# A decoder kernel's gated feed-forward: gate and up from split one-pass parts, the weight parts made in the stage before it and streamed by tile, and the scan's C rows spread from one 128-row tile

## The reference, cut to what matters

```
w = lut[idx]                                    # gate, up and down each look their weights up
gate = x @ w_gate.T;  up = x @ w_up.T           # 512 -> 1376
h = silu(gate) * up
out = h @ w_down.T                              # 1376 -> 512

state = state * exp(delta_t * A) + (delta_t * u_t) * B_t      # 16 states x 512 channels, 512 steps
y_t = sum over n of state[n] * C_t[n]
```

## Time and profile before

| | us |
|---|---|
| median of 3 runs | 2576.68 (2576.60 to 2576.71) |
| the profiled execution, its own time | 2584.38 |
| its span, first to last instruction | 2582.6 |
| context stage in that span | 930 to 1198 |
| feed-forward and scan | 1198 to 1865 |

### The profile page before, as it was taken

How to read it: one execution, slowest core, us unless ns; L and a number is a source line. 1 busy time by engine, 2 the same in 40 slices (tenths; PEclk the granted TensorE clock), 3 DMA queues, 4 the chain that set the end, 5 groups by cost and what they waited for, 6 DMA issues and landing times. The chain is left out here.

```text
span 2582.6 us, 24445 instructions
## 1 busy us (share of the span) xinstructions
PE 2262.6 (88%) x6992; PEld 1049.2 (41%) x6992; DVE 1771.1 (69%) x2979; ACT 920.4 (36%) x1759; POOL 1052.6 (41%) x789
## 2 busy tenths in 40 slices
PE   6998998999899777774798989989869999999858
PEld 3554444455455443332243434334333333434224
DVE  1887687688768877773688897987745455554454
ACT  1443323334333323331554636446203323232311
POOL 2453333355333424443598888988700000000033
PEclk9999999999999988886899999999979999999878
DMA  6000000000000022225321222221142222121021
GB/s 245 18 21 17 17 25 21 17 17 21 21 17 25 22 88 82 82 82 198 116 91 53 86 83 82 91 77 62 49 131 50 50 49 49 40 58 34 16 98 53
DMA packets 88746, 158.34 MB, mean 61 GB/s; under 512 B 14912, under 2 KB 42432, under 8 KB 86352
## 3 DMA queue, kind: packets, MB, share of 16 engines
q1 hardware_dynamic: 72256, 139.76, 17.1%
q10 hardware_dynamic: 15888, 17.43, 2.1%
q0 software_dynamic: 512, 0.13, 0.0%
HBM read 101.18 MB, written 30.80 MB: 51 GB/s over the span
## 5 line engine op out<-in xcount | busy, mean ns | idle before, releaser
L1389 PE MATMUL c_bank<-c_xn_t,c_weights 128*128 128x512 f32 (+1 forms) x704 | 326.4, 609 | 21.1 <-ACT c_h_t L1429 19.5
L706 POOL TENSOR_SCALAR a_prob<-a_prob,a_rsum 128x256 f32<-128x256 f32 x256 | 147.1, 594 | 466.8 <-DVE a_rsum L634 466.6
L1287 DVE TENSOR_TENSOR_SCAN s_state<-s_decay,s_state 128x512 f32<-128x512 f32 x256 | 305.0, 1210 | 36.1 <-ACT s_decay L1221 36.1
L1237 POOL TENSOR_TENSOR s_state<-s_b_rows,s_delta_u 128x1024 f32<-128x1024 f32 x128 | 301.2, 2363 | 11.2 <-DMA s_b_rows<-scan_bc 8.8
L1221 ACT ACTIVATE s_decay<-s_delta,s_a 128x512 f32<-128x512 f32 x256 | 173.2, 688 | 296.5 <-DVE s_state L1287 269.4
L438 PE MATMUL a_bank<-a_xn_t,a_wq 128*128 128x512 f32 x512 | 227.2, 592 | 0.0
L521 PE MATMUL a_bank<-a_wo,a_out_t 128*128 128x512 f32 x512 | 222.3, 592 | 0.0
L1910 POOL DMA_DIRECT2D d_qs<-d_neg_t x16 | 8.2, 514 | 515.3 <-DVE d_neg_t L1841 515.3
L549 ACT ACTIVATE a_prob<-a_score,a_neg_m 128x256 f32<-128x256 f32 x256 | 117.8, 476 | 278.8 <-DVE a_neg_m L629 278.6
L320 DVE TENSOR_SCALAR f_picks<-f_mask,f_lut_xor,f_lut 128x260 int32<-128x260 int32 x512 | 202.5, 468 | 9.6 <-DVE f_mask L314 1.1
L1762 ACT ACTIVATE d_prob_t<-d_score 128x512 f32<-128x512 f32 x256 | 139.0, 595 | 194.5 <-PE d_score L1645 193.2
(11 more groups left out here) (194 smaller groups left out, 3726.6 us busy)
## 6 DMA issues: line engine op xcount, KB each, us to landing
s_b_rows<-scan_bc SPq DMA_DIRECT2D x64, 512.0 KB, 3.6
f_idx<-in_idx SPq DMA_DIRECT2D x64, 130.0 KB, 2.1
ffn_weights<-f_picks SPq DMA_DIRECT2D x64, 130.0 KB, 1.8
...
d_qs<-d_hi SPq DMA_DIRECT2D x128, 64.0 KB, 2.0
d_ks<-d_hi SPq DMA_DIRECT2D x128, 64.0 KB, 2.0
...
```

Of the source, the lines that this page charges most:

```text
L1237: pool.tensor_tensor(self.state[:, s], row.broadcast_to([P, 2, T]), self.delta_u[:, h % 2], ALU.mult) \
L1287: dve.tensor_tensor_scan(self.state[:, s, e, :], self.decay[u % 2][:], self.state[:, s, e, :], 0.0, ALU.mult, ALU.add).then_inc(self.scann ...
L1389: mm = nc.tensor.matmul(banks[b][0:width[o], :], weights[:, lo:lo + width[o]], xn_t[:, k, :], start=(k == 0), stop=(k == KD - 1))
```

## The change

1. **Parts of the weights.** A class `WeightSplit` runs in the context stage. The 11008 gate and up columns are cut into 16 pieces of 688, four in each pass. For each: SP loads it, ACT rounds it to float32r (`hi`), POOL subtracts (`lo`), SP stores both to two new DRAM tensors. Pieces 0 and 1 of a pass stand on ACT between the copies of the attention and the SiLU of `u`, on POOL between the factor adds and `d_u`; pieces 2 and 3 stand on both at the end of the pass. On SP the loads of 0 and 1 stand behind the factors' loads, and the stores of 2 and 3 at the end, ahead of the next pass's factors. To make room, `one_e` now lies in `conv`, and `delta` in `log1p`.
2. **Fills.** x is split the same way (ACT rounds out of PSUM, DVE subtracts). A fill is twelve float32r matmuls: for each k, hi x hi, hi x lo and lo x hi; lo x lo is left out. The weights of a tile `o` come as two DMAs of 512 KB into one of four slots, the first by SP, all others by ACT, in each of the four passes anew: `load_ahead` behind each `gate`. The down weights stay in SBUF in float32 as before, from one DMA.
3. **Order of the pieces.** The features of the next pass move from piece 34 to piece 28, between the second and the third down tile; the statistics and the normalization move to pieces 8 and 12, among the fills. The last down tile's add comes at the end of the pass.
4. **C.** All four batches' C rows, twice, are loaded into one 128-row tile at the stage's start by eight DMAs, rounded and split once; `spread_c` picks one of 64 columns. The split in each pass is gone.

The diff, cut to its core:

```diff
+class WeightSplit:
+    PER_PASS = 4
+    SW = W_DOWN // (B * PER_PASS)
...
+    def load(self, sp, i, n):
+        if n >= 2:
+            sp.wait_ge(self.subtracted[n % 2], self.turn(i, n))
+        sp.dma_start(self.raw[:, n % 2, :].bitcast(I32), self.scratch["weights"][:, self.columns(i, n)]) \
+            .then_inc(self.raw_in[n % 2], 16)
+    def round(self, act, i, n):
+        act.wait_ge(self.raw_in[n % 2], self.turn(i, n) * 16 + 16)
+        act.wait_ge(self.stored[n % 2], self.turn(i, n) * 32 + 1)
+        self.nc.scalar.copy(self.hi[:, n % 2, :], self.raw[:, n % 2, :]).then_inc(self.rounded[n % 2], 1)
...
 def stage_context ... sync
+                split.load(sp, i, 0)
+                split.load(sp, i, 1)
...
+                for n in range(2):
+                    split.store(sp, i, n)
+                    split.load(sp, i, n + 2)
...
+                for n in range(2, 4):
+                    split.store(sp, i, n)
 stage_ffn
-    STATS_AT, NORM_AT = FILLS + 2, FILLS + 6
+    XN_AT = FILLS + 2 * PARTS
+    STATS_AT, NORM_AT = 8, 12
...
-                for k in range(KD):
-                    lo = b * W_UP + k * INTER + o * P
-                    mm = nc.tensor.matmul(banks[b][0:width[o], :], weights[:, lo:lo + width[o]], xn_t[:, k, :],
-                                          start=(k == 0), stop=(k == KD - 1))
+                terms = [(k, w, x_) for k in range(KD) for w, x_ in ((0, 0), (0, 1), (1, 0))]
+                for k, w, x_ in terms:
+                    at = (b * KD + k) * width[o]
+                    mm = nc.tensor.matmul(banks[b][0:width[o], :], w_parts[:, n % SLOTS, w, at:at + width[o]],
+                                          xn_parts[:, x_, k, :],
...
+            for n in range(1, SLOTS):
+                load_ahead(n)
             scan.scalar_setup(act)
             features(0)
-            for o in range(EARLY, OT):
-                load_weights(act, o)
+            act.dma_start(w_down[:].bitcast(I32), ...)
...
                     if j < FILLS and j % 2 == 1:
                         gate(i, j // 2)
+                        if i * OT + j // 2 >= 1:
+                            load_ahead(i * OT + j // 2 + SLOTS - 1)
 class Scan
-        self.nc.tensor.matmul(self.c_bank[c % 2][:], self.c_pick[:, n:n + 1].broadcast_to([2 * DS, P]),
-                              self.c_parts[:, i % 2, :], start=True, stop=True).then_inc(self.c_spread, 1)
+        self.nc.tensor.matmul(self.c_bank[c % 2][:], self.c_pick[:, n:n + 1].broadcast_to([P, P]),
+                              self.c_parts[:], start=True, stop=True).then_inc(self.c_spread, 1)
```

199 lines of the change are left out of this document (125 added, 74 removed).

## The result

| | us (median) | us (range) | profiled execution: us / span |
|---|---|---|---|
| before | 2576.69 | 2576.60 to 2577.45 | 2584.4 / 2582.6 |
| after | 2531.85 | 2530.08 to 2534.32 | 2532.93 / 2531.1 |

The ratio is 0.983 (95% interval 0.981 to 0.984): 44.8 us faster. I had forecast 19.5 us. The two traces differ by more, 51.5 us of span, because the profiled execution before lay 7.7 us over its median and the one after 1.1 over. No view shows what the 7.7 us are, but the clock goes with them: of the other executions of the kernel before on record, those of 2582 us and more had a mean granted clock of 0.935 to 0.938, those under 2580 one of 0.938 to 0.942, and the profiled one had 0.937. All of the 51.5 us lie in the two changed stages (943.1 us before, 891.5 after).

The account below looks back on a forecast made before the run. PE bounds the fills, POOL and DVE close behind. Start -23.3, pass 0 +1.6, passes 1 and 2 -2.5 together, pass 3 -8 make -32; context +12.5; total -19.5 from 2576.7, 2557 us, range 2522 to 2582.

Parts of the forecast that it names:

- The start: Start of the feed-forward: ACT issues one load before the first decay, not eighteen; first scan 23.3 us earlier.
- Context: Context stage: weight split adds 12.5 us, +2.5 in three passes, +2 in the first, +3 for last stores.
- The norm among the fills: Fills: normalization 7.4 and statistics 3.6 make 11 us of DVE; 3 us more for the clock, in each of three passes.
- Stalls at the gates: Fills: DVE stands still 1.15 us at 28 gates, 0.7 from the table loads' chain and 0.4 from DMA issues.
- The downs: Down stretch of a pass: 50.9, plus 3 for features and 3.6 of PE idle, 57.5 us against 62.9.
- PE's piece: Fills: twelve matmuls in 2.82 us and a spread of 0.24; a piece falls from 4.05 to 3.06 us.
- DVE's waits for a fill: Start of a pass's fills: PE needs 6.4 us before the first lift, DVE has 4.1 of work, 2.3 idle.
- the full gain: Rival, chance 0.14: gate stalls don't appear in the fills, ACT running ahead; 32 us less, 2525 us.
- Context eats it: Rival, chance 0.10: rounding late in all context passes, +29 in place of 12.5, fills gain 4 less; 2578 us.
- A fall of the clock: Rival, chance 0.05: PE's granted clock falls to 1.2 GHz among fills, half the pieces slow, 79 us more; 2636 us.
- the held issues: Rival, chance 0.09: ACT's DMA issues behind gates held by a full queue, 1.4 us more a pair; 2600 us.

Follow-up runs that it names:

- the best with three terms: Changed kernel with GpSimd's factor sums, then subtractions of pieces 0 and 1 behind d_u, ScalarE's roundings behind the SiLU, factor sum stored from ScalarE's queue: 2491.35 us, 0.965.

## Why the prediction was wrong

The direction and the range held (2522 to 2582), the size didn't: 44.8 us, not 19.5. By the stage marks the change brings -51.7 where -19.5 was forecast, and the difference lies in pass 0 (-7.2, forecast +1.6) and passes 1 and 2 (-30.9 together, forecast -2.5); the start and the context stage were each worse than forecast, by 2 and 6. So the steps that failed are those of a pass: the norm's length, the stalls at the gates and the downs. By the prediction's own steps:

- **The start, -23.3.** Measured -21.3 (42.5 to 21.2). Right, within 2. POOL got its B rows 18.7 us after the stage's start, behind the 4 MB of weights, where 17 was forecast.
- **Context, +12.5.** Measured +18.3: passes +0.9, +3.8, +5.2, +4.4 and the end +4.0. The mechanism was named, and two of its operations were in the wrong place: I let two subtractions hold the convolution at its start for 1.7 us (it was 0.4) and overlooked that the other two stand right behind the factor sums, at the convolution's end, and hold it for 2 x 1.4 us. ACT's rounding ended at 1095.06 in pass 2, where the forecast had 1091 "just in time"; the last SiLUs waited for DVE all the same.
- **The norm among the fills, 11 us and 3 for the clock.** This step failed worst. I took 7.4 us from the earlier trace rows as the operations' length. It was 1.9 of work and 5.5 of being held beside GpSimd's operations, and the earlier trace rows had shown me just that one stage earlier. Measured 1.9 and 2.5, with the small operations some 4.9 in all: 6 us less in each of three passes. That GpSimd rests at piece 12 was luck: the prediction didn't look, and at piece 16 it doesn't. The clock I had half right. Three passes have a norm among their fills, 0 to 2. In pass 0 the granted clock fell to 1.2 GHz twice for 3.4 us, each time within 1 us of the end of a pause of PE (2.4 and 2.1 us) at the norm's two places; over the fills of pass 0 it was 0.94. In passes 1 and 2 PE paused as long, and the clock stayed at 1.00: 3 us less in each of the two.
- **Stalls at the gates, 1.15 us at 28.** The tables' part was right (0.7, measured 0.7); the issues' 0.4 was not (most issues are done ahead of the gate, as ACT's timeline and the run with twice the issues show), and 17 gates had a stall, not 28. 12.5 us in place of 32; and by the run without tables only 3 to 8 of these 12.5 were on the path.
- **The downs, 57.5.** Measured 53.3, since the C spread saves 0.39 us twelve times, 4.7 us, and I had given it nothing there. The idle time of PE for the features' subtraction was 3.3 us (forecast 3.6). The last pass's downs had nothing of the saving: 51.9, forecast 50. There PE waited 2.8 us for a weighing and the granted clock lay at 1.2 GHz for 6.8 us.
- **PE's piece.** 12 matmuls follow each other in 2.8 us, as forecast, but with the spread behind them a piece takes 3.3 to 3.5 us from start to start at most places and not 3.06. Here 3.53:

```profile
1420.80 2.96 PE L1460 MATMUL c_bank<-c_xn_parts,c_w_parts 128*128 128x512 f32 x12
1423.82 0.50 PE L1242 MATMUL s_c<-s_c_parts,s_c_pick 128*128 128x512 f32 x1
1424.33 3.04 PE L1460 MATMUL c_bank<-c_xn_parts,c_w_parts 128*128 128x512 f32 x12
```

  What makes the difference of 0.2 to 0.5 is open. And the statement "PE is the engine to relieve" with three terms as the means was half of it: the cheaper spread alone brings the float32 piece from 4.05 to 3.66 us, and DVE and the gates need about that.
- **Against it**, DVE's waits for a fill didn't go: 5.5 us in the fills of passes 1 to 3 and 11.4 in pass 0, where I had 2.3.

For passes 1 and 2: 157.5 forecast, 143.3 measured. Of the 14.2, norm 6, clock 3, stalls 4 (6.9 less 2.9), downs 4.2, less 3 for the waits. Of the rivals, the full gain (2525) came nearest. Its reason, stalls that don't appear, held for 20 of its 32 us; the rest came from the norm and the downs, which it didn't name, and was partly eaten by the waits for PE, so that its figure is near by luck. "Context eats it" had the direction of that stage's error right (18.3, between 12.5 and 29). A fall of the clock over much of the fills was seen only with one term, and the held issues only with loads over 43 and 42 partitions. By the rule of the Trainium skill (ScalarE: Activation LUTs, "What ACT_TABLE_LOAD costs") each switch of tables would cost a further 1.38 us. The trace doesn't agree: ACT's timeline again shows the next activation 0.01 us behind the load.

The clock's 3 us were not wrong for every execution. Passes 1 and 2 of some three-term kernels took 146.5 and 144.9 us in place of 143.3, with the same code in this stage, and in them the clock fell as forecast. The stretch of statistics and normalization in pass 1 of after, then two stretches from the same place in the best with three terms:

```profile
1414.80:1445.00 30.20, 24.47 (x96) 17.15 (x94) 26.28 (x35) 18.31 (x23) 24.11 (x12) 1.00 0.67 244
```

```profile
1375.80:1379.20 3.40, 3.26 (x8) 2.61 (x9) 3.40 (x5) 2.12 (x3) 3.23 (x2) 0.50 0.97 360
1392.90:1396.30 3.40, 3.40 (x6) 1.37 (x5) 3.40 (x4) 2.83 (x4) 3.32 (x2) 0.50 0.53 152
```

PE's pauses ahead of them are the same in both, 2.2 and 2.1 us. Left open: why the clock falls behind them in one execution and not in the other, and what the profiled execution before had over its median beyond its lower clock.
